# Sampling stage of a convolution, attention and expert kernel: a quarter of the one-hot clips moves from ScalarE to VectorE, and the sums over points from one VectorE reduction to a VectorE halving and GpSimd adds

## What is computed

```
v   = value.reshape(4, 256, 8 heads, 16)
off = query @ soff_w + soff_b                 # 8 heads x 8 points x (x, y)
aw  = softmax(query @ attw_w + attw_b)        # 8 heads x 8 points
sampled = bilinear(v, px, py)                 # map of height 256 and width 1
out[q, head] = sum over 8 points of aw * sampled
```

## Time and profile before

| | us |
|---|---|
| median of 3 runs | 288.53 |
| the 3 runs | 290.47, 288.53, 283.49 |
| the profiled execution | 284.63 |
| its span, first to last instruction | 282.8 |
| VectorE, ScalarE, TensorE, GpSimd busy | 210.1, 177.7, 228.8, 50.0 |

### The profile page before, as it was taken

The page is one execution under the profiler, slowest core; times in us unless marked ns, Lnnn a source line. Parts: engine busy times, 40 slices in busy tenths (PEclk is TensorE's granted clock), DMA queues, the critical chain, the costliest instruction groups (busy, mean ns, idle before and its releaser), DMA issues.

```text
span 282.8 us, 7527 instructions
## 1 busy us (share of the span) xinstructions
PE 228.8 (81%) x2908; PEld 158.0 (56%) x2908; DVE 210.1 (74%) x481; ACT 177.7 (63%) x260; POOL 50.0 (18%) x64
## 2 busy tenths in 40 slices
PE   0899469999999998769999568999876605999984
PEld 0579237676767677547989456666544404233352
DVE  4757887999999999874245877888747979697512
ACT  8678979898989897058343567566673232566510
POOL 7004939800000000010002000000000277500000
PEclk9999959999999999987999999999999555799999
DMA  6920000000000000690000000000009515130002
GB/s 144 378 94 2 1 0 2 0 2 0 0 0 0 0 0 2 241 351 4 0 3 0 0 0 2 2 0 2 1 2 370 234 48 163 44 112 2 0 2 74
DMA packets 8836, 16.15 MB, mean 57 GB/s; under 512 B 752, under 2 KB 5104, under 8 KB 8432
## 3 DMA queue, kind: packets, MB, share of 16 engines
q1 hardware_dynamic: 8304, 14.83, 15.0%
q0 software_dynamic: 512, 1.05, 1.2%
HBM read 12.73 MB, written 3.15 MB: 56 GB/s over the span
## 4 chain that ended last, share of the span: by engine, by line
PE 63%; DVE 12%; ACT 9%; issue 7%; DMA 4%; POOL 2%; SPq 1%; POOLq 0%; DVEq 0%; ACTq 0%
PE ps L1275 12%; PE ps L1259 9%; PE ps L1569 8%; ACT arena L574 3%; DVE t_k L972 3%; PE ps L1342 3%; PE ps L1425 2%; PE ps L1374 2%; POOL slot_rows L490 2%; PE ps L1386 2%; PE ps L1588 2%; PE ps L1163 2%; DMA r_sb<-in_rows 2%; PE ps L1332 2%; PE ps L1398 2%
## 5 line engine op out<-in xcount | busy, mean ns | idle before, releaser
L574 ACT ACTIVATE arena<-ps,one_less_sq 128x1024 bf16<-128x1024 f32 x64 | 68.7, 1114 | 7.3 <-PE ps L1259 7.0
L1275 PEld LDWEIGHTS ps<-arena 128*128 128x128 bf16 x1536 | 47.6, 96 | 19.7 <-issue 7.4
L1275 PE MATMUL ps<-arena 128*128 (+1 forms) x1536 | 50.4, 184 | 2.2 <-ACT arena L574 2.1
L1259 PE MATMUL ps<-wide,sel 128*128 (+1 forms) x128 | 39.2, 390 | 8.1 <-ACT arena L574 6.1
L931 DVE TENSOR_REDUCE msda<-wide 128x768 f32 x32 | 45.3, 1458 | 0.0
L926 DVE TENSOR_TENSOR wide<-ps,wide 128x768 f32<-128x768 f32 x32 | 29.8, 955 | 4.0 <-PE ps L1275 4.0
L490 POOL DMA_INDIRECT slot_rows<-nrm,slots x16 | 16.5, 1034 | 72.6 <-DVE slots L1067 68.0
L1569 PE MATMUL ps<-arena,w_sb 128*32 x48 | 23.3, 632 | 0.0
L972 DVE TENSOR_REDUCE t_k<-ps 128x2 f32<-128x512 f32 x32 | 20.5, 683 | 0.0
L643 ACT ACTIVATE wide<-ps 128x512 f32<-128x512 f32 x32 | 17.3, 595 | 1.4 <-PE ps L1410 1.3
L1574 PE MATMUL ps<-late,w_sb 128*32 128x512 f32 x80 | 16.5, 662 | 0.0
(11 more groups left out here) (298 smaller groups left out, 497.3 us busy)
## 6 DMA issues: line engine op xcount, KB each, us to landing
arena<-in_w_t SPq DMA_DIRECT2D x1, 4096.0 KB, 15.0
wide<-in_w_t SPq DMA_DIRECT2D x1, 2048.0 KB, 8.0
slot_rows<-t_c SPq DMA_DIRECT2D x2, 768.0 KB, 9.9
wide<-in_w_t SPq DMA_DIRECT2D x1, 1536.0 KB, 11.3
late<-slot_rows SPq DMA_DIRECT2D x6, 256.0 KB, 3.6
w_sb<-in_weights SPq DMA_DIRECT2D x1, 1480.0 KB, 8.3
x_sb<-in_x SPq DMA_DIRECT2D x4, 128.0 KB, 2.3
wide<-in_w_t SPq DMA_DIRECT2D x1, 512.0 KB, 8.0
```

Of the source, the lines that this page charges most:

```text
L574: nc.scalar.activation(hot[:, u, 2 * c:2 * c + 2, :, :], ps[:, 2 * (c % 2):2 * (c % 2) + 2, :].rearrange("r p (b q) -> r p b q", b=B), ACT ...
L1259: ins = nc.tensor.matmul(ps[:, 2 * (c % 2) + p % 2, :], sel[:, bass.ds(i % 4, 1), p, :].rearrange("k h j -> k (h j)"), terms_t[:, bass.ds( ...
L1275: ins = nc.tensor.matmul(ps[:, 4 + b, p * NK * DH:(p + 1) * NK * DH], hot[:, u, p, b, :], rhs, start=(s == 0), stop=(s == PARTS - 1))
```

## The change

On ScalarE only three of the four clips of a step remain. The fourth (points 6 and 7) is done on VectorE, by `last_one_hot`: a tensor_scalar (add the bias, then max with 0) from PSUM to bfloat16. So that no engine must negate, the selector `sel` gets the other sign, with `twice_j` in the place of `minus_2j` and `sel_low` negated; these are the same number of instructions as before.

The reduction L931 goes away. In its place VectorE adds the two halves of a product's 24 terms (`halve`: 384 columns, both inputs in SBUF), into a new buffer `part_sums` with two halves, one for each u. GpSimd does the rest for all four tiles at once (`sums`): additions of 384, 192, 64 and 64 columns, each waiting for the one before, the last into `msda`. The halving of step s waits for the sums of step s - 2.

VectorE's order in a step becomes: product 0, clip of step s+1, product 1, halving 0, halving 1. The very first clip, `last_one_hot(0, 0)`, stands behind the preparation of the weights. The sixteen weight-parting instructions of GpSimd are spread over the steps, one ahead of each step's sums. TensorE waits for ScalarE's three clips (`hot_ready`) and VectorE's (`last_hot`) apart. VectorE's loop has seven rounds instead of eight, with the last two steps written out.

The diff, cut to its core:

```diff
 prod = hat_y[:, :, :, :].rearrange("q k t r -> q (k t r)").rearrange(
     "q (s b n d) -> q s b n d", s=2, b=2, d=DH)
+part_sums = wide[:, 0:2 * B * NK * NP // 2 * DH].rearrange("q (u b n d) -> q u b n d", u=2, b=B, d=DH)
 msda = sb("msda", [P, TILES, NH, DH])
...
-HOT_CREDIT, G_CREDIT, FREE_CREDIT = 2, 3, 2
+HOT_CREDIT, G_CREDIT, FREE_CREDIT, SUM_CREDIT, HALVED_CREDIT = 1, 3, 2, 2, 1
...
+def part_weights(n):
+    w, high, low, parted = ((W("geglu"), geglu_h, geglu_l, geglu_parted),
+                            (wqk, wqk_h[:, :], wqk_l[:, :], wqk_parted))[n // 8]
+    m = n // 2 % 4
+    cols = slice(m * quarter, (m + 1) * quarter)
+    if n % 2 == 0:
+        nc.gpsimd.tensor_tensor(high[:, cols], w[:, cols], one_c[:, 0:1].to_broadcast([P, quarter]),
+                                ALU.mult).then_inc(parted, 1)
+    else:
+        pool.wait_ge(parted, 2 * m + 1)
+        nc.gpsimd.tensor_tensor(low[:, cols], w[:, cols], high[:, cols].bitcast(F32),
+                                ALU.subtract).then_inc(parted, 1)
+def sums(step):
+    i, u = step // 2, step % 2
+    part = part_sums[:, u, :, :, :]
+    pool.wait_ge(halved, 2 * step + 2 + HALVED_CREDIT)
+    nc.gpsimd.tensor_tensor(part[:, :, 0:6, :], part[:, :, 0:6, :], part[:, :, 6:12, :],
+                            ALU.add).then_inc(sum_step, 1)
+    pool.wait_ge(sum_step, 3 * step + 1)
+    nc.gpsimd.tensor_tensor(part[:, :, 0:3, :], part[:, :, 0:3, :], part[:, :, 3:6, :],
+                            ALU.add).then_inc(sum_step, 1)
+    pool.wait_ge(sum_step, 3 * step + 2)
+    nc.gpsimd.tensor_tensor(part[:, :, 0, :], part[:, :, 0, :], part[:, :, 1, :], ALU.add).then_inc(sum_step, 1)
+    pool.wait_ge(sum_step, 3 * step + 3)
+    nc.gpsimd.tensor_tensor(msda[:, u:u + 7:2, i, :], part[:, :, 0, :], part[:, :, 2, :],
+                            ALU.add).then_inc(sums_ready, 1)
 pool.wait_ge(ld_wc, 16)
 pool.wait_ge(wk3_ready, NK)
-wqk = w_sb[:, WAT["wq"][0]:WAT["wk"][1]]
-quarter = 2 * GE * P // 4
-for w, high, low, parted in ((W("geglu"), geglu_h, geglu_l, geglu_parted),
-                             (wqk, wqk_h[:, :], wqk_l[:, :], wqk_parted)):
-    for n in range(4):
-        cols = slice(n * quarter, (n + 1) * quarter)
-        nc.gpsimd.tensor_tensor(high[:, cols], w[:, cols], one_c[:, 0:1].to_broadcast([P, quarter]),
-                                ALU.mult).then_inc(parted, 1)
-        pool.wait_ge(parted, 2 * n + 1)
-        nc.gpsimd.tensor_tensor(low[:, cols], w[:, cols], high[:, cols].bitcast(F32),
-                                ALU.subtract).then_inc(parted, 1)
+for step in range(2 * NH):
+    part_weights(step)
+    sums(step)
...
-def one_hots(i, u, which=range(NP // 2)):
...
-ACT.Relu, scale=-1.0, bias=one_less_sq[:, 0:1]).then_inc(hot_ready, 1)
+ACT.Relu, bias=one_less_sq[:, 0:1]).then_inc(hot_ready, 1)
...
-one_hots(0, 0, range(1, 4))
+one_hots(0, 0, range(1, 3))
...
-with dve.Fori(0, NH) as i:
+def last_one_hot(i, u):
+    dve.wait_ge(g_ready, 4 * i + 2 * u + 1)
+    dve.wait_ge(dist_mm, 8 * i + 4 * u + 4)
+    nc.vector.tensor_scalar(hot[:, u, NP - 2:NP, :, :],
+                            ps[:, 2:4, :].rearrange("r p (b q) -> r p b q", b=B),
+                            one_less_sq[:, 0:1], 0.0, ALU.add, ALU.max).then_inc(last_hot, 1)
+def weigh(i, u, c):
+    dve.wait_ge(g_ready, 4 * i + 2 * u + c + 1 + G_CREDIT)
+    g = ps[:, 4 + 2 * c:6 + 2 * c, 0:NP * NK * DH].rearrange("q b (n d) -> q b n d", d=DH)
+    w = wk3[:, 4 * c + u:4 * c + u + 3:2, bass.ds(i * NP, NP), :].rearrange("q b p k -> q b (p k)")
+    nc.vector.tensor_tensor(prod[:, c, :, :, :], g,
+                            w.unsqueeze(3).to_broadcast([P, 2, NP * NK, DH]),
+                            ALU.mult).then_inc(g_free, 1)
+def halve(i, u, c):
+    n = NP * NK // 2
+    dve.wait_ge(g_free, 4 * i + 2 * u + c + 1 + FREE_CREDIT)
+    nc.vector.tensor_tensor(part_sums[:, u, 2 * c:2 * c + 2, :, :], prod[:, c, :, 0:n, :], prod[:, c, :, n:2 * n, :],
+                            ALU.add).then_inc(halved, 1)
+def weighted(i, u, last):
+    if u == 0:
+        dve.wait_ge(halved, 4 * i + HALVED_CREDIT)
+    else:
+        dve.wait_ge(halved, 4 * i + 2 + HALVED_CREDIT)
+    weigh(i, u, 0)
+    if u == 0:
+        last_one_hot(i, 1)
+    elif not last:
+        last_one_hot(i + 1, 0)
+    weigh(i, u, 1)
+    dve.wait_ge(sums_ready, 2 * i + u + 1)
+    halve(i, u, 0)
+    halve(i, u, 1)
+last_one_hot(0, 0)
+with dve.Fori(0, NH - 1) as i:
     for u in range(2):
-        for c in range(2):
-            dve.wait_ge(g_ready, 4 * i + 2 * u + c + 1 + G_CREDIT)
-            dve.wait_ge(prod_free, 4 * i + 2 * u + c + 1)
-            g = ps[:, 4 + 2 * c:6 + 2 * c, 0:NP * NK * DH].rearrange("q b (n d) -> q b n d", d=DH)
-            w = wk3[:, 4 * c + u:4 * c + u + 3:2, bass.ds(i * NP, NP), :].rearrange("q b p k -> q b (p k)")
-            nc.vector.tensor_tensor(prod[:, c, :, :, :], g,
-                                    w.unsqueeze(3).to_broadcast([P, 2, NP * NK, DH]),
-                                    ALU.mult).then_inc(g_free, 1)
-        for c in range(2):
-            dve.wait_ge(g_free, 4 * i + 2 * u + c + 1 + FREE_CREDIT)
-            nc.vector.tensor_reduce(msda[:, 4 * c + u:4 * c + u + 3:2, bass.ds(i, 1), :].rearrange(
-                                        "q b h d -> q b (h d)"),
-                                    prod[:, c, :, :, :].rearrange("q b n d -> q b d n"),
-                                    AX_X, ALU.add).then_inc(prod_free, 1)
+        weighted(i, u, False)
+for u in range(2):
+    weighted(NH - 1, u, True)
...
-pe.wait_ge(hot_ready, 8 * i + 4 * u + c + 1)
+if c == 1:
+    pe.wait_ge(last_hot, 2 * i + u + 1)
+else:
+    pe.wait_ge(hot_ready, 6 * i + 3 * u + max(c, 1))
...
-pe.wait_ge(hot_ready, 8 * i + 4 * u + 4 + HOT_CREDIT)
+pe.wait_ge(hot_ready, 6 * i + 3 * u + 3 + HOT_CREDIT)
+pe.wait_ge(last_hot, 2 * i + u + 2)
...
-pe.wait_ge(prod_free, 4 * NH + FREE_CREDIT)
+pe.wait_ge(sums_ready, 2 * NH + SUM_CREDIT)
```

More of the change, by code:

```diff
@@ L110, in build @@
         sel_low = sb("sel_low", [P, 4, NP])
-        minus_2j = sb("minus_2j", [P, P])
+        twice_j = sb("twice_j", [P, P])
         w_sb = sb("w_sb", [P, WTOTAL])
@@ L300, in build @@
         terms_ready, terms_mm, terms_t_ready, wk3_ready = sems("terms_ready terms_mm terms_t_ready wk3_ready")
-        dist_mm, hot_ready, g_ready, g_free, prod_free = sems("dist_mm hot_ready g_ready g_free prod_free")
-        msda_mm, msda_c_ready, out_mm, t1_ready, t1_mm, t1_c_ready = sems(
-            "msda_mm msda_c_ready out_mm t1_ready t1_mm t1_c_ready")
+        dist_mm, hot_ready, last_hot, g_ready, g_free, halved, sums_ready = sems(
+            "dist_mm hot_ready last_hot g_ready g_free halved sums_ready")
+        sum_step, msda_mm, msda_c_ready, out_mm, t1_ready, t1_mm, t1_c_ready = sems(
+            "sum_step msda_mm msda_c_ready out_mm t1_ready t1_mm t1_c_ready")
         geglu_parted, hn_h_ready, hn_l_ready, wqk_parted, z1_h_ready, z1_l_ready = sems(
@@ L456, in _ @@
             hat(hat_y[:, 2, :, :], y_rest[:, :, :], 2, spare, 2, hat_y2_ready)
+            wqk = w_sb[:, WAT["wq"][0]:WAT["wk"][1]]
+            quarter = 2 * GE * P // 4
+            def part_weights(n):
[10 more added lines that the diff above has]
+                                            ALU.subtract).then_inc(parted, 1)
@@ L514, in selectors @@
                     at = 4 * NP * h + p
-                    ins = nc.scalar.activation(sel[:, h, p, :], minus_2j[:, :], ACT.Identity,
+                    ins = nc.scalar.activation(sel[:, h, p, :], twice_j[:, :], ACT.Identity,
                                                scale=ident[:, at:at + 1], bias=sel_low[:, h, p:p + 1])
@@ L565, in _, with one_hots @@
             first_part(3, VALUE_ORDER[3])
-            def one_hots(i, u, which=range(NP // 2)):
+            def one_hots(i, u, which=range(NP // 2 - 1)):
                 act.wait_ge(g_ready, 4 * i + 2 * u + 1)
@@ L789, in _ @@
             by_term = ident[:, :].rearrange("k (h c p) -> k h c p", h=4, c=4)
-            nc.vector.tensor_tensor(sel_low[:, :, :], by_term[:, :, 1, :], by_term[:, :, 2, :],
-                                    ALU.add).then_inc(sel_low_ready, 1)
+            nc.vector.scalar_tensor_tensor(out=sel_low[:, :, :], in0=by_term[:, :, 1, :], scalar=-1.0,
+                                           in1=by_term[:, :, 2, :], op0=ALU.mult, op1=ALU.subtract).then_inc(sel_low_ready, 1)
             for b in range(B):
@@ L842, in _ @@
             nc.vector.memset(gap[:, 2:3], 0.0).then_inc(g_free, FREE_CREDIT)
-            nc.vector.memset(gap[:, 3:4], 0.0).then_inc(prod_free, FREE_CREDIT)
+            nc.vector.memset(gap[:, 3:4], 0.0).then_inc(sums_ready, SUM_CREDIT)
+            nc.vector.memset(gap[:, 4:5], 0.0).then_inc(last_hot, 1)
+            nc.vector.memset(gap[:, 5:6], 0.0).then_inc(halved, HALVED_CREDIT)
             for h in range(2):
```

2 lines of the change are left out of this document (1 added, 1 removed).

## The result

The changed kernel takes 299.02 us in the median of 4 runs (294.49 to 299.66), beside 286.41 us for the kernel before (283.49 to 290.47; a fourth run of it, 284.30, has joined the three of the table above). The ratio is 1.0407, with a 95% interval from 1.0333 to 1.0481: it is slower by 4%, where 291.0 us and a range from 286 to 297 were forecast. The ratios and their intervals leave out executions that ran long at a lower granted clock, as 6 of 32 further ones of the kernel before did (292.65 to 293.67 us at a mean clock of 0.887 to 0.894; the other 26 took 283.43 to 286.52 at 0.922 to 0.939), so a ratio need not be the quotient of the medians, here 1.044. The profiled execution took 299.24 us.

The account below looks back on a forecast made before the run. The prediction took a circle of clip, gathers and distances as the bound, not VectorE. Start 4.5, circle 0.5 and 0.2, end 0.4 gave +5.6 us: 290.2 from the profiled execution, 294.1 from the median; 291.0 was named, range 286 to 297.

Parts of the forecast that it names:

- What bounds the kernel: Sampling loop: a circle of waits through three engines sets the 4.71 us step, though VectorE is busy 54.30 of 56.56 us.
- The circle: Sampling steps: VectorE's clip of 1.22 us replaces ScalarE's 1.11; +0.5 us in the loop, +0.2 in two steps without branch.
- The start: First gather: waits for VectorE's weight preparation and clip, starts at 44.05 instead of 39.97; +4.1 us, carried to the end.
- the term for the clock: Start of sampling: TensorE idles and restarts from the low clock level; +0.3 us taken, bounds 0 and +0.8.
- with 0.18 us to spare: Loop steps set by TensorE's branch (4.68 us): the longer clip fits in the spare time and costs 0.
- the sign of being right: Sampling loop: 4.7 to 4.8 us from one step's first gather to the next, VectorE idle before products.
- VectorE's covers: Sampling step: VectorE is free 0.25 us before the clip, and its halvings end at 1.9 us, before the product at 2.05.
- GpSimd: Sampling steps: sums take about 2.5 us, 3.2 with weight parting, under 4.7; hidden in every step but the last.
- The end: From the last step's first gather to the transposes: 8.2 us instead of 7.80; +0.4, bounds -0.2 and +1.8.
- three small items: Behind the transposes: bias on x and memset shift on GpSimd, load of w1 5 us later; each 0.
- GpSimd rival: Sampling loop: sums over 3.0 us block VectorE's halvings, 0.4 us a step, +5.6 more, 296 us; chance 0.16.
- the bound: Whole kernel: about 2% (5.7 us) is what a measurement can tell from no change; the sum was +5.6.

Follow-up runs that it names:

- all_clips_scalar: The changed kernel with all four clips of each step on ScalarE, halvings and GpSimd's sums kept; 288.21 us, ratio 1.001 to the kernel before.
- after_again: The changed kernel unaltered, measured once more; 297.22 us, no ratio, with the kernel before at 285.06 us beside it.
- late_start: The kernel before with one added wait: TensorE starts the sampling loop only after VectorE's last preparation; 291.51 us, ratio 1.019.
- late_wait_scalar: Changed kernel, all clips on ScalarE, TensorE's wait for the fourth clip moved ahead of a gather's last 6 matmuls; 280.84 us, 0.990 of the kernel before.
- delay_1: The kernel before with one unused VectorE multiplication of 1024 columns ahead of the transposes; 291.53 us, ratio 1.021.

## Why the prediction was wrong

- **What bounds the kernel: right.** The circle of clip, gathers and distances, and not VectorE, set the pace; all_clips_scalar shows it with 20 us of VectorE's work gone and no change.
- **The start: right in mechanism and size of the wait** (+4.1 forecast; G(0,0) 4.55 later, of which 0.42 come from all earlier work being that much later in this profile). Wrong in the term for the clock in this profile: +0.3 was taken, bounds 0 and 0.8, and step 0 took 1.48 more, of which about 0.17 are the longer clip. In after_again it took only 0.28 more (6.06), as forecast. The term was tied to TensorE's idle time, and the runs show no such tie: late_start's step 0, behind a longer wait, took 5.47.
- **The circle: a step of the argument failed.** The sum said that every other step is set by TensorE's branch "with 0.18 us to spare", so that a longer clip would cost nothing there. But both kinds of step grew alike, 4.68 to 4.85 and 4.74 to 4.93. The row at 69.29 of the earlier trace rows follows the end of the clip (69.03) by 0.26 us, and in the changed kernel the gather at 66.41 follows the clip's end at 66.14 by 0.27: the gather waits for the clip in both, only with a longer way from signal to start where the branch lies between. Behind the branch the gather follows the distance by 0.57 us before (68.72 to 69.29) and by 0.74 in the changed kernel (65.67 to 66.41), but by 0.44 in late_wait_scalar, where it does not wait for the last clip. From signal to start I had assumed about 0.1 behind the branch too, as in the other step. And the clip took 1.284 instead of 1.22: 0.17 more than ScalarE's 1.112, in all 14 steps 14 x 0.17 = 2.4 of the 2.6 us measured (2.12 + 0.50), where the sum had 0.7. The pace of 4.89 lies above the 4.7 to 4.8 that was named as the sign of being right.
- **VectorE's covers: right.** It idles 0.3 to 0.4 us ahead of each clip and never holds up TensorE with a product or halving.
- **GpSimd: right.** 1.001, 0.594 and 0.32 us for 384, 192 and 64 columns are 2.1 ns a column and 0.19 fixed, 2.24 us a step; with the gaps between them a step's sums take 2.48 (63.30 to 65.78), about the 2.5 forecast. It is hidden in all steps but the last. The end cost +0.14 instead of +0.4. There the halvings and the sums met: L488 took 0.67 instead of 0.32, the two halvings 1.14 instead of 1.02. The loop shows no such case. The Trainium skill (SBUF — State Buffer, section Who interferes with whom) describes a lock between such instructions; these rows agree with it.
- **Behind the sampling: the step that failed most.** The sum ended at the transposes; it named three small items behind them, each at 0, and gave the clock there no term at all. The rest took +5.8 us in the first profile and +2.9 in the second. With the measured +8.8 up to the transposes alone the time would have been 284.63 + 8.8 = 293.4, within the range. The range reached up to 297 only by way of a GpSimd rival that did not happen.

The sum with measured terms: 4.55 + 1.48 + 2.62 + 0.14 = 8.8 up to the transposes, against 5.6 forecast, and 3 to 6 behind. The chance for slower, 0.46, stood next to 0.48 for no change, since the sum lay on the bound; the circle and what came behind the sampling pushed it over in both profiles.

## What to carry to other kernels

Ask of a nearly full engine whether it is full because it is slow or because a circle of waits through several engines lets it run just so often; a kernel that takes a third of its work away tells it in one run, and the cut belongs where the circle closes (here a wait moved by 18 matmuls took 2.4 us off twelve steps, though nothing off the whole kernel by itself, and VectorE's relief was worth 1 us only after it). An operation moved onto such a circle is paid at the difference of the two engines' prices in each turn, and its first instance at whatever its new queue still has to do. The last item in a helper engine's queue should be the one that is waited for.

## What the runs showed of the hardware

- A delay of 1.2 us ahead of the middle of this kernel costs 5.9 us, of 2.4 us 4.8, of 3.5 us 8.0. In delay_1 TensorE's granted clock comes out lower in code that is the same (0.86 and 0.92 instead of 0.91 and 1.00). A difference of 1 to 2% between two versions of this kernel is not proof of their work; the starts of marked instructions in the trace are the safer measure.
- A clip of 1024 columns from PSUM with a bias held in SBUF takes 1.284 us on VectorE, 0.17 more than ScalarE's 1.112. The tensor_scalar of 256 columns without such a bias (0.424) with 768 more at 1.065 ns would have given 1.24.
- Twelve matmuls that do nothing, in a wait of 4 us, made the next step 1.1 to 2.3 us shorter (4.92 instead of 6.06 and 7.26 in the two profiles of the changed kernel).
